# Second cross attention of a four-layer stack: the limits in one VectorE pass, the maximum subtracted on GpSimd, and a new order of the work

## The chip, the cores and the metric

The kernel runs on one core of one Trainium2 chip. The metric is the device time of one execution in microseconds (us). TensorE does the matrix products, VectorE, ScalarE and GpSimd the rest; SyncE issues most transfers. In the rows they are PE (with PEld, its weight loads), DVE, ACT, POOL and SP.

## The reference

A batch of 32 samples with 128 tokens and 256 features goes through four cross attentions (L0 to L3), each followed by a feed-forward part of its own kind. Every attention has 16 heads. The change touches the third of them, which is called L2:

```python
x = x + tanh(g_xattn[2]) * L2_xattn(layernorm(x), ctx_768, ...)

def L2_xattn(query, key_value, ...):          # 16 heads of 16 features, 128 queries, 128 keys
    attn = einsum('bhqd,bhkd->bhqk', q, k) * scale      # scale = 16 ** -0.5
    attn = clip(attn, -10000, 10000)
    attn = softmax(attn, axis=-1)
    attn = where(any(isnan(attn)), 1 / Nkv, attn)
    out  = einsum('bhqk,bhkd->bqhd', attn, v)
    return out @ Wo + bo
```

The L2 feed-forward part is a causal self attention followed by a gated two-matrix part ("self" in the kernel); L3 is another cross attention, with a stack of three residual blocks behind it ("L3f").

## The kernel before

**Lanes and passes.** Four lanes each carry one sample at a time through the stages, in eight passes. The first half of the program runs L0, "bit", L1 and "route" for all passes (FIRST), the second half "mix", L2, "self" and L3 (SECOND). A closing part, L3f, runs eight lanes over four passes. Each lane owns two PSUM pairs of banks and SBUF buffers of its own, so lanes meet only on the engines: each engine takes the steps of all lanes in one fixed sequence, and a step that isn't ready holds up everything behind it on that engine.

**What sets the order.** Each engine's program is a set of generators, one for each lane, that yield after a step. `turns` (a loop over the characters of `ORDER[engine]`) takes the next step of the lane that the next digit names: 0 to 3 are the four lanes, 4 is the set-up work, further characters the eight lanes of L3f. The strings for pe, dve, act, pool and sp have 3,624, 3,963, 3,022, 1,372 and 341 characters. Signals are semaphores that count the steps told, so that the strings may be permuted only between lanes, and every wait holds whatever the order.

**One round of L2.** `dve_heads`, `pool_heads`, `act_heads` and `pe_heads` handle eight heads at a time, two rounds for each sample. In a round TensorE writes the scores of eight heads (line 453 in `pe_heads`, signal s). VectorE takes the maximum of each query and head over the keys (line 796, one instruction over 128x1024 numbers, signal top) and, in L2 alone, clamps these 8 maxima in the small tile `top` (line 800, signal clip). Then for each half c of the round, four heads or 128x512 numbers, three engines follow each other on the tile `t.e[c]` ("big" in the rows):

```python
# VectorE, line 812: max(scores, -limit) - clamped maximum
dve.scalar_tensor_tensor(t.e[half], s8[:, mine, :], -CLAMP / DH ** -0.5, shift, ALU.max, ALU.subtract)
# GpSimd, line 1496: min(that, 0), in place
pool.tensor_scalar(e, e, 0.0, None, ALU.min)
# ScalarE, line 1310: exp(scale * that), in place
act.activation(flat, flat, ACT.Exp, scale=DH ** -0.5)
```

With the minimum against 0 the upper limit is kept: a score above the limit has a clamped maximum equal to the limit. TensorE then transposes the half (line 424), for which it waits for ScalarE's signal p and, at c = 0, for VectorE's second half too. ScalarE copies the transposed halves out of PSUM (line 1269), and after the second round TensorE multiplies by the values (line 469). In "self" and L3 GpSimd has no part in this: VectorE subtracts (line 815) and ScalarE goes on at once. L1's softmax has a GpSimd step of another kind: line 1519 multiplies a 128x512 half by a broadcast reciprocal, tensor by tensor. In all cross attentions and in "self" GpSimd also builds the masked keys (line 1488, 128x512, two instructions for a sample, tensor by tensor), adds a bias to x (line 1506), and computes the norms' reciprocal roots (lines 1471 and 1473; 1527 and 1529 in "self"). On VectorE, line 786 applies a norm, lines 1045, 1052 and 1053 are steps of "self" on 128x256 numbers that lie in SBUF.

Of the kernel before, what the change touches and what calls it, by code (L numbers as in the profile page):

```python
# [10 lines left out]
ALU = mybir.AluOpType  # L11
# [4 lines left out]
P = 128  # L16
# [139 lines left out]
def sequence_a(n):  # L156

    for half in (FIRST, SECOND):
# [8 lines left out]
        "3221131321321342331112232111133212122343200213111300000333021321221011011101033010313313113213200103"  # L167
        "2112123312022323333312132312311222022021233101213001310310032201132331232310132102122331010200031121"
        "1233000302232330220201201332321011301022112102000011100121121102132200130123022033211303302321211002"
        "0022233121213123302031310103011331220321122101201230312323320021031132133000223002303022023321120030"  # L170
        "1002133012202020313113010301101201233033211121100120123022032031131311323300231201021222231322132313"
        "3130333101223102003311221310233210201203232332113131300220200000003320231203301230310302321100322122"
        "1100103303110121112110021012201202303202030331103223312300211002222331212131233133103303122302110220"
        "1303200211031331220102120230003110122100023303223322032031213010013312322023013101301000211333310021"
        "1110211210021023023202030321123123113322312212221213300003122333121232303310123120220331012313321023"
        "0310101221332101311302232020023203202310003123220313211030131030021321010200133020320321120021011212"
        "1200111303201203030310132100300113233223122122101231301301310013033033011223100202231122121201032121"
        "0321200211311332200230030330223320320321012002123011330221212310011303130333120312031203322003301112"
        "1121001201302203020303311020320032122211222213012033113102101023312312320333112032103232113200212012"
        "1332313322002110113000000303302232302320120133001311220202330103113013030012012333130011110211010220"  # L180
        "1230220320311332100200123122322323120120120100131232103200221013313332330101231012021001020203320301"
        "3322123113001102233202032323010101130232311221221033101022322310103102213112001120313323210133120102"
        "1330222213312221332231232313211212313311333121330321200302030112312002300131210012013301301201233023"
        "0031030311122031213030030221130210212020233211301012033123132300132131302201113220303022011130131322"
        "1010213212203103232220112233130032211323010210230132012031123313102000302013313310322032301013212300"
        "2021120133012021320102012003320212300302230021030111301312230201132113232300211201331310012020233020"
        "3102201310310322311322011101013221312001201312320033120120213302022330220231312231230231021030100211"
        "2310013002213120013022330201120123332302021130130312023102132002310111001130230230211003311223200320"
        "1312320033013013210322120223300312011011233103223011102231123120012023332321330022201313021330220203"
        "1312231031021030312003133210031331002233320013322002110321232301122133120301012000323000322130120311"  # L190
        "0311203201132110302301213200101013301032022121112023301303202313221001102212312002323030233021201001"
        "3322213312221330231213013012310100321321003333200232133131002230201132012032321120133010031202103230"
        "0032210320311103112203211032113232311001033123001202010330323103103122011130302231223113300221013231"
        "2330021020331032023222201132223102003031020123323300210013330221302303131022310202133210201300002321"
        "1300213230231310122012103310322023213002120113311320022202233101301122302211301312201213203232310133"
        "0211211220010331121010320302202101231320321132132030110022312313300221331200120012323300330121302103"
        "2032120330031000212330002113001301322130123230321323100103312302221102332031103112320322110101021231"
        "3321032133201111203311120013103212212201330220311023130202113210132313132030322002333220083237287200"
        "328003783789a700a78330a90378a09807a89339873930703a38007098ac97ba908ba98ac0070b7800cab8ca89bc78bc0980"
        "7807acb89ab8c7ba908ba8c07acab7097ba97a890a8ca90bc7070b08a90ab9cb8956bc6b9875c7a6c8c6ab5c965b95ba65cb"  # L200
        "a6c57656ca9565bc9b68756a5c897cb7869685ba95c69c6a6b5a6c5bcabc5976c5b9a6576956597578a68cb659b57c976ca6"
        "5c5bb6ac68c598659b56a5b7a87ca685c6569a565b98b78697c657bc5abc9b6786abca75867568a768b695b7bc5895acb958"
        "6c97c65a6b956575c9b6c565"
    ),
    "dve": (
        "1132322030141341331242424111323324121444144121244111311132202113232313132130230031311212310110111301"
        "3121331233233113032313033100302323230202022020202123322202331112120320200003030311200101030011010011"
        "1220112123331311033303333331011222203323222221122211111110113331212121030131202230131313331313123121"
        "1322121002021222201330303020010100310222221020022322232122320300223323331130303311220022000030030003"
        "1110310200011101100111000010002003201112201113322221331222200211122201110211331331333333332221301111"  # L210
        "2122313300102110121113133000222012222221000120002020233022112331031002233323232322203230130332323323"
        "1103330313312032303200031200000011133111131001112300100202003210010120003301301310022221123222223322"
        "3112100333331333111113202101233311210122111001310313101132321100103332223032323223232010000020020221"
        "1221213322020202321223323002023323131333300323123012302300000000033101303211001111011010121203020020"
        "0001113000333222021112222220022012031331113112111213320331333131312220011013133202111112113312321002"
        "2022212102230030020200203201313221213333330200232232233132000332233213133030313202133000200000002003"
        "0000000031112013101330110110220300012001021000000301022120100020033212230122301222020333113223332331"
        "1310033111011113202211333121211120212122321232132121121001130232012222321210202023230220303030303000"
        "3230111132200022333003103332232333233003131003101000030003300110100120330011101133010100100112202003"
        "2111001110022223320220321122223121211111111022211331313222333131313030133030122111111220200112023332"  # L220
        "2222010000200112032332221210332121032222332233333323000232303013303223331303031333010203230100200032"
        "0030002001311001000011121200101211332011331222112003022022112122233223311002202111033111131132112201"
        "1331313333300130110223131312212112200122013320213200001020202202332101032313213323323230003223213300"
        "0323323232110033313331202300020323000030000101012001030101031101003201321110120201111020223010112122"
        "2313221223220321111222120033303202232331333333132200010222333032002110100300303301122210000123312210"
        "1003033113321211120203330121000021020000000020002000030303022121012333222110311313311330220213111333"
        "0200211121020202331130201131303101221303023230300322321210100033332211212020202333321100013313331133"
        "2223100010122000112133311000220221112232330002021311332302011020012013312100313132020303321111332220"
        "0011113223300121003221323100202001222123130001223202031313103320211012233233020210133213300010213310"
# [1249 lines left out]
def pool_heads(pool, m, t, p, l):  # L1479
# [666 lines left out]
```

## Time and profile before

| | us |
|---|---|
| median of 3 runs | 2675.64 |
| lowest and highest of them | 2671.07 and 2676.82 |
| the profiled execution: its own time | 2694.11 |
| the profiled execution: its span, first to last instruction | 2692.9 |

The profiled execution is 18.5 us longer than the median, and its own time is 1.2 us more than its span. In it TensorE was busy for 2484.1 us, VectorE for 1967.9, ScalarE for 1667.6 and GpSimd for 1327.8. A busy TensorE is not TensorE at its peak, since the ends of matrix products are modelled in the profile. A group of rows gives, for a line, an engine and an operation, the number of instructions, their busy time, the mean of one, and the time that the engine sat idle just before them with what ended it. The chain of waits is followed back from the last instruction, at each step to what released it.

### The profile page before, as it was taken

How to read it: one execution, taken by the hardware profiler on the slowest of the kernel's cores; microseconds unless marked ns; L12 is line 12 of the kernel's file. 1: busy time of each engine (PE TensorE's matmuls, PEld its weight loads, DVE VectorE, ACT ScalarE, POOL GpSimd, SP SyncE). 2: the span in 40 equal slices, each digit the busy share in tenths (PEclk: the TensorE clock that was granted, in tenths of full speed). 3: DMA queues.
4: the chain of work that ended last, by engine and by line, in shares of the span. 5: the costliest groups of instructions: out<-in, count | busy, mean ns of one | idle time of the engine just before them, and what ended most of it. 6: DMA issues, size and time to landing. Idle time of an engine off the chain costs nothing.

```text
span 2692.9 us, 66669 instructions
## 1 busy us (share of the span) xinstructions
PE 2484.1 (92%) x26500; PEld 2026.9 (75%) x26500; DVE 1967.9 (73%) x4666; ACT 1667.6 (62%) x4537; POOL 1327.8 (49%) x2117
## 2 busy tenths in 40 slices
PE   6899989898899999998899989999999989999999
PEld 4777767786677777777677777787777868788887
DVE  7778787869687786966565656667766676668998
ACT  4676767676567667765465555656566565666644
POOL 3232334242544434355664664545545464645777
PEclk9899999999899999999999999999999999999999
DMA  6000000000012221000111221100000000000010
GB/s 197 5 26 8 23 9 21 17 18 15 23 54 60 71 58 41 23 25 17 27 50 50 75 78 31 38 28 19 20 17 20 18 21 18 25 6 25 30 38 28
DMA packets 84191, 92.51 MB, mean 34 GB/s; under 512 B 15333, under 2 KB 77289, under 8 KB 83881
## 3 DMA queue, kind: packets, MB, share of 16 engines
q1 hardware_dynamic: 75432, 59.91, 7.2%
q0 software_dynamic: 8448, 28.34, 3.7%
q8 instruction: 210, 3.44, 0.5%
q14 instruction: 101, 0.82, 0.1%
HBM read 65.36 MB, written 22.85 MB: 33 GB/s over the span
## 4 chain that ended last, share of the span: by engine, by line
PE 48%; DVE 24%; POOL 13%; ACT 9%; issue 4%; DMA 2%; another core or an unknown queue 1%; SPq 0%; DVEq 0%; POOLq 0%; ACTq 0%
PE psum L376 12%; PE psum L369 8%; POOL big L1496 6%; PE psum L404 5%; PE psum L453 5%; DVE tiny L796 4%; PE psum L424 3%; PE psum L597 2%; PE psum L469 2%; ACT big L1310 2%; PE psum L383 2%; PE psum L397 2%; DVE big L815 2%; ACT big L1353 2%; PE psum L591 2%
## 5 line engine op out<-in xcount | busy, mean ns | idle before, releaser
L1310 ACT ACTIVATE big<-big 128x512 f32<-128x512 f32 x512 | 313.1, 630 | 211.3 <-DVE big L815 118.5
L796 DVE TENSOR_REDUCE tiny<-psum 128x8 f32<-128x1024 f32 x256 | 311.7, 1219 | 118.3 <-PE psum L453 112.1
L1471 POOL TENSOR_SCALAR tiny<-mv 128x1 f32<-128x1 f32 x224 | 56.9, 254 | 559.1 <-DVE mv L776 556.8
L424 PEld LDWEIGHTS psum<-ident,big 64*128 64x128 f32 x5120 | 208.6, 141 | 137.7 <-ACT big L1310 72.6
L424 PE MATMUL psum<-ident,big 64*128 64x64 f32 x5120 | 254.4, 232 | 62.2 <-ACT big L1310 41.5
L453 PE MATMUL psum<-head_keys,small 64*128 64x256 f32 x2048 | 286.0, 400 | 21.6 <-POOL head_keys L1488 8.0
L1488 POOL TENSOR_TENSOR head_keys<-big,head_rows 128x512 f32<-128x512 f32 x256 | 267.0, 1052 | 0.2
L815 DVE TENSOR_TENSOR big<-psum,tiny 128x512 f32<-128x512 f32 x384 | 251.3, 682 | 3.4
L1519 POOL TENSOR_TENSOR big<-big,tiny 128x512 f32<-128x512 f32 x128 | 135.1, 1061 | 233.6 <-DVE tiny L851 233.1
L1269 ACT ACTIVATE big<-psum 128x512 f32<-128x512 f32 x384 | 213.1, 600 | 59.7 <-PE psum L424 57.5
L1496 POOL TENSOR_SCALAR big<-big 128x512 f32<-128x512 f32 x128 | 190.8, 1503 | 115.2 <-DVE big L812 115.0
L453 PEld LDWEIGHTS psum<-head_keys,small 64*128 64x128 f32 x2048 | 180.7, 190 | 69.2 <-issue 17.7
L1353 ACT ACTIVATE big<-psum,tiny 128x128 f32<-128x128 f32 x512 | 181.2, 381 | 31.1 <-DVE tiny L846 28.5
L404 PE MATMUL psum<-ident,small 128*128 128x128 f32 x896 | 158.5, 286 | 28.0 <-ACT small L1320 7.7
L1269 ACT ACTIVATE head_keys<-psum 128x512 f32<-128x512 f32 x256 | 141.6, 597 | 47.5 <-PE psum L424 46.6
L786 DVE TENSOR_SCALAR xn<-x,mv,tiny 128x256 f32<-128x256 f32 x192 | 101.1, 528 | 76.1 <-POOL tiny L1473 75.2
L404 PEld LDWEIGHTS psum<-ident,small 128*128 128x128 f32 x896 | 99.6, 142 | 69.2 <-ACT small L1320 15.4
L1473 POOL TENSOR_TENSOR tiny<-tiny,minus_half 128x1 f32<-128x1 f32 x224 | 130.3, 582 | 18.7
L369 PE MATMUL psum<-xnT,w_L 128*128 128x128 f32 x1024 | 132.1, 280 | 1.1 <-ACT xnT L1340 0.5
L369 PEld LDWEIGHTS psum<-xnT,w_L 128*128 128x128 f32 x1024 | 126.3, 195 | 6.6 <-issue 2.8
L369 PE MATMUL psum<-xnT,w_up 128*128 128x128 f32 x1024 | 129.8, 278 | 0.0
L597 PE MATMUL psum<-w_L,head_keys 128*128 128x256 f32 x512 | 128.3, 389 | 0.8 <-ACT head_keys L1362 0.5
(340 smaller groups left out, 6638.1 us busy)
## 6 DMA issues: line engine op xcount, KB each, us to landing
ctxT<-in_ctxT SPq DMA_DIRECT2D x64, 128.0 KB, 2.2
after_L_xattn<-x SPq DMA_DIRECT2D x64, 128.0 KB, 1.7
mixture_out<-spare SPq DMA_DIRECT2D x46, 128.0 KB
x_in<-in_x SPq DMA_DIRECT2D x32, 128.0 KB
mixture_in<-xn SPq DMA_DIRECT2D x32, 128.0 KB, 1.7
x_in<-after_L_xattn SPq DMA_DIRECT2D x32, 128.0 KB
w_bits<-after_L_xattn SPq DMA_DIRECT2D x32, 128.0 KB, 2.2
spare<-in_L_w SPq DMA_DIRECT2D x2, 1024.0 KB, 6.4
```

What stands on the lines that cost most here:

```text
L369: last = pe.matmul(bank[:, j * S:(j + 1) * S], wt[:, k, n * P:(n + 1) * P], src[:, k, :], start=k == 0, stop=k == KD - 1)
L376: last = pe.matmul(bank[:, 0:n], srcT[:, k, :], wt[:, k, 0:n], start=k == 0, stop=k == chunks - 1)
L404: last = pe.transpose(bank[:, k * P:(k + 1) * P], src[:, k * P:(k + 1) * P], identity)
L424: last = pe.transpose(t.ab[:, half, at:at + P // 2], t.e[c][rows, j, :], m.ident[rows, rows])
L453: last = pe.matmul(t.ab[:, half, cols], t.qT[rows, r, :], keys[rows, cols], start=l != "self", stop=l != "self" or cols.start > 0)
L796: dve.tensor_reduce(top, s8, AX.X, ALU.max).then_inc(*t.dve.tell(p, f"{l}.top{r}"))
L815: dve.tensor_tensor(t.e[half], s8[:, mine, :], shift, ALU.subtract).then_inc(*t.dve.tell(p, f"{l}.e{2 * r + half}"))
L1269: return act.activation(dst.rearrange("p h (r s) -> p h r s", r=2), src, ACT.Copy)
L1310: last = act.activation(flat, flat, ACT.Exp, scale=DH ** -0.5)
L1353: last = act.activation(t.e[half][:, j, :], t.ab[:, half, j * S:(j + 1) * S], ACT.Exp, scale=WIDE ** -0.5, bias=t.tiny[:, 8 + h:9 + h], ac ...
L1488: pool.tensor_tensor(t.head_keys[r], t.kT[:, r:r + 1, :].to_broadcast([P, CH, S]), m.head_rows[:].rearrange("p (h o) -> p h o", o=1).to_br ...
L1496: pool.tensor_scalar(e, e, 0.0, None, ALU.min).then_inc(*t.pool.tell(p, f"{l}.below{c}"))
```

## The change

In L2 alone VectorE's pass keeps both limits and no longer subtracts: it takes max(score, -limit) and then the minimum of that and the clamped maximum. GpSimd's step takes two tensors instead of a tensor and a constant: it subtracts the clamped maximum, which is read from the small tile and broadcast over the keys. The number of instructions and the signals stay the same. The order strings of all five engines are other ones; every step of every lane is still there.

```diff
 ORDER = {
     "pe": (
-        "3221131321321342331112232111133212122343200213111300000333021321221011011101033010313313113213200103"
...
+        "2311323312131224111332231121313212123243202011311300020030321313201011012111300301313131131233021030"
...
@@ dve_heads
             if l == "L2":
-                dve.scalar_tensor_tensor(t.e[half], s8[:, mine, :], -CLAMP / DH ** -0.5, shift, ALU.max, ALU.subtract
+                dve.scalar_tensor_tensor(t.e[half], s8[:, mine, :], -CLAMP / DH ** -0.5, shift, ALU.max, ALU.min
                                          ).then_inc(*t.dve.tell(p, f"{l}.e{2 * r + half}"))
@@ pool_heads
     if l == "L2":
         for c in range(4):
-            e = t.e[c % 2].rearrange("p h s -> p (h s)")
+            top = t.tiny[:, 8 + CH * (c % 2):8 + CH * (c % 2 + 1)].rearrange("p (h o) -> p h o", o=1)
             pool.wait_ge(*t.dve.at(p, f"{l}.e{c}"))
-            pool.tensor_scalar(e, e, 0.0, None, ALU.min).then_inc(*t.pool.tell(p, f"{l}.below{c}"))
+            pool.tensor_tensor(t.e[c % 2], t.e[c % 2], top.to_broadcast([P, CH, S]), ALU.subtract
+                               ).then_inc(*t.pool.tell(p, f"{l}.below{c}"))
             yield
```

Of the steps, the places in the strings differ like this: on TensorE 1,463 of 3,624 stand elsewhere, mostly by one or two places and by 11 at most; on GpSimd 882 of 1,372, by 15 at most, and on SyncE by up to 18. The changes are spread over the whole program, not over L2 alone. The added line moves the lines behind it by one, so that 1506 is now 1507, 1527 now 1528 and 1609 now 1610, while the changed GpSimd instruction is still at line 1496.

**Place 1: TensorE, second round of L2 of lane 0 in an early pass.** A number behind a name is the lane. Before, from the scores of lane 0 (line 453, head_keys_0) to the transposes of both its halves (line 424, big_0) and on:

```order
L453 MATMUL psum<-head_keys_0,small_0 128x256 x4
L424 MATMUL psum<-ident,big_1 128x64 x16
L369 MATMUL psum<-xnT_2,w_up 128x128 x8
L424 MATMUL psum<-ident,big_3 128x64 x16
L453 MATMUL psum<-head_keys_1,small_1 128x256 x4
L469 MATMUL psum<-big_3,small_3 32x128 x8
L469 MATMUL psum<-head_keys_3,small_3 32x128 x8
L424 MATMUL psum<-ident,big_0 128x64 x16
L404 MATMUL psum<-ident,small_3 128x128 x4
L376 MATMUL psum<-w_down,big_2 128x256 x6
```

Of the change, the same stretch:

```order
L453 MATMUL psum<-head_keys_0,small_0 128x256 x4
L424 MATMUL psum<-ident,big_1 128x64 x8
L369 MATMUL psum<-xnT_2,w_up 128x128 x8
L424 MATMUL psum<-ident,big_3 128x64 x8
L453 MATMUL psum<-head_keys_1,small_1 128x256 x4
L424 MATMUL psum<-ident,big_3 128x64 x8
L376 MATMUL psum<-w_down,big_2 128x256 x3
L469 MATMUL psum<-big_3,small_3 32x128 x8
L469 MATMUL psum<-head_keys_3,small_3 32x128 x8
L376 MATMUL psum<-w_down,big_2 128x256 x3
L404 MATMUL psum<-ident,small_3 128x128 x4
L424 MATMUL psum<-ident,big_1 128x64 x8
```

Behind the last of these rows stand the halves of lane 0, one at a time, with a half of lane 1 between them. The six products with w_down and the four transposes of small_3 now stand between lane 0's scores and its transposes, where they came behind these before.

**Place 2: GpSimd, the same round of lane 0.** Before:

```order
L1554 TENSOR_TENSOR tiny_2<-tiny_2 128x1
L1488 TENSOR_TENSOR head_keys_1<-big_1,head_rows 128x512
L1496 TENSOR_SCALAR big_0<-big_0 128x512 x2
L1506 TENSOR_TENSOR x_1<-x_1,out_bias_L3 128x256
L1506 TENSOR_TENSOR x_0<-x_0,out_bias_L2 128x256
L1609 DMA yg_1<-mixture_out0,token_place0 128x256
```

Of the change:

```order
L1530 TENSOR_TENSOR tiny_2<-tiny_2,minus_half 128x1
L1496 TENSOR_TENSOR big_0<-big_0,tiny_0 128x512
L1507 TENSOR_TENSOR x_1<-x_1,out_bias_L3 128x256
L1610 DMA yg_1<-mixture_out0,token_place0 128x256
L1496 TENSOR_TENSOR big_0<-big_0,tiny_0 128x512
L1507 TENSOR_TENSOR x_0<-x_0,out_bias_L2 128x256
```

The two halves of lane 0 stood back to back; now a bias and the issue of an indirect transfer stand between them. Over the program 7 of the 64 pairs had other work between their halves, and now 6 have.

**Place 3: TensorE at the start of the program, in L0, which the two edits don't touch.** Before:

```order
L404 MATMUL psum<-ident,xn_1 128x128 x2
L404 MATMUL psum<-ident,xn_3 128x128 x2
L404 MATMUL psum<-ident,xn_2 128x128 x2
L369 MATMUL psum<-xnT_1,w_L0q 128x128 x4
L369 MATMUL psum<-xnT_3,w_L0q 128x128 x4
L369 MATMUL psum<-xnT_2,w_L0q 128x128 x4
```

Of the change:

```order
L404 MATMUL psum<-ident,xn_3 128x128 x2
L369 MATMUL psum<-xnT_3,w_L0q 128x128 x4
L404 MATMUL psum<-ident,xn_1 128x128 x2
L404 MATMUL psum<-ident,xn_2 128x128 x2
L369 MATMUL psum<-xnT_1,w_L0q 128x128 x4
L453 MATMUL psum<-head_keys_3,small_3 128x256 x4
```

Lane 3 now goes ahead of lane 1, and the scores of lane 3 come ahead of lane 2's queries.

## Rows read from the trace of the kernel before

**Rows 1.** The page's first part and its row of TensorE's granted clock in 40 slices.

```profile
PE 2484.1 (92%) x26500; PEld 2026.9 (75%) x26500; DVE 1967.9 (73%) x4666; ACT 1667.6 (62%) x4537; POOL 1327.8 (49%) x2117
...
PEclk9899999999899999999999999999999999999999
```

**Rows 2.** Busy time by windows: stretch, its length, PE, PEld, DVE, ACT, POOL, granted clock.

```profile
0.00:1157.00 1157.00, 1047.31 (x11848) 844.53 (x11849) 910.01 (x2379) 774.50 (x2362) 435.31 (x689) 0.96 0.13 39
1157.00:2400.00 1243.00, 1150.30 (x12702) 944.88 (x12702) 804.36 (x1560) 730.98 (x1777) 699.06 (x1032) 0.99 0.11 31
2400.00:2693.00 293.00, 286.51 (x1954) 237.46 (x1952) 253.51 (x728) 162.07 (x399) 193.41 (x398) 1.00 0.09 28
```

**Rows 3.** TensorE's waits, 1157 to 2400: total us, times, longest.

```profile
PE psum L424 <- ACT big L1310: 34.3, 57, 1.0
...
PE psum L404 <- DVE small L1045: 7.1, 8, 2.1
PE psum L404 <- DVE xn L786: 5.7, 7, 1.8
```

**Rows 4.** The chain of waits by line, 1157 to 2400.

```profile
by line: POOL big L1496 12.9%; PE psum L376 10.9%; PE psum L369 8.6%; PE psum L453 7.7%; DVE tiny L796 7.1%; PE psum L404 5.1%; issue 4.3%; PE psum L424 4.0%; ACT big L1310 3.2%; PE psum L469 3.0%; DVE big L812 2.8%; POOL head_keys L1488 2.
```

**Rows 5.** Line 1496's own instructions, and ScalarE's waits for it, 1157 to 2400.

```profile
L1496 POOL TENSOR_SCALAR big<-big x128: 1475/1496/1750, 1167.4 to 2398.8; 128x512 f32<-128x512 f32 x128
...
ACT big L1310 <- POOL big L1496: 90.8, 102, 2.7
```

**Rows 6.** Timeline: start, us, instruction, idle before it; place 1 and 2 before.

```profile
1456.69 0.69 DVE L812 SCALAR_TENSOR_TENSOR big<-psum,tiny 128x512 f32<-128x512 f32 x1
...
1457.47 2.96 POOL L1496 TENSOR_SCALAR big<-big 128x512 f32<-128x512 f32 x2 [0.84 <-DVE big L812]
...
1460.45 0.63 ACT L1310 ACTIVATE big<-big 128x512 f32<-128x512 f32 x1 [0.82 <-POOL big L1496]
...
1461.14 0.46 PE L424 MATMUL psum<-ident,big 64*128 64x64 f32 x8 [0.83 <-ACT big L1310]
```

**Rows 7.** GpSimd's groups: line 1519 from the page, the others 1157 to 2400.

```profile
L1519 POOL TENSOR_TENSOR big<-big,tiny 128x512 f32<-128x512 f32 x128 | 135.1, 1061 | 233.6 <-DVE tiny L851 233.1
...
L1488 POOL TENSOR_TENSOR head_keys<-big,head_rows 128x512 f32<-128x512 f32 x184 | 191.5, 1050 | 0.2
L1496 POOL TENSOR_SCALAR big<-big 128x512 f32<-128x512 f32 x128 | 190.8, 1503 | 115.2 <-DVE big L812 115.0
...
L1506 POOL TENSOR_TENSOR x<-x,out_bias_L 128x256 f32<-128x256 f32 x60 | 44.1, 738 | 0.3
```

**Rows 8.** The longest of line 1519, and VectorE's passes over 128x512 scores.

```profile
L1519 POOL TENSOR_TENSOR big<-big,tiny x128: 1031/1041/1397, 93.9 to 1209.7; 128x512 f32<-128x512 f32 x128
...
L815 DVE TENSOR_TENSOR big<-psum,tiny 128x512 f32<-128x512 f32 x235 | 153.8, 681 | 2.2
L812 DVE SCALAR_TENSOR_TENSOR big<-psum,tiny 128x512 f32<-128x512 f32 x128 | 84.7, 685 | 1.7
```

**Rows 9.** VectorE on SBUF operands: groups of 1157 to 2400, then least, median, most.

```profile
L786 DVE TENSOR_SCALAR xn<-x,mv,tiny 128x256 f32<-128x256 f32 x96 | 53.2, 554 | 47.2 <-POOL tiny L1473 46.8
...
L1053 DVE SCALAR_TENSOR_TENSOR x<-xn,gates,x 128x256 f32<-128x256 f32 x30 | 19.1, 635 | 0.0
L1052 DVE TENSOR_SCALAR small<-xn,tiny 128x256 f32<-128x256 f32 x30 | 17.9, 598 | 19.6 <-POOL tiny L1529 19.5
...
L786 DVE TENSOR_SCALAR xn<-x,mv,tiny x192: 321/412/1240, 53.1 to 2496.8; 128x256 f32<-128x256 f32 x192
...
L1052 DVE TENSOR_SCALAR small<-xn,tiny x32: 325/354/1232, 1249.0 to 2469.6; 128x256 f32<-128x256 f32 x32
...
L1053 DVE SCALAR_TENSOR_TENSOR x<-xn,gates,x x32: 472/480/1257, 1249.2 to 2469.9; 128x256 f32<-128x256 f32 x32
```

**Rows 10.** Timeline of one such pass beside GpSimd's masked keys.

```profile
1408.91 1.05 POOL L1488 TENSOR_TENSOR head_keys<-big,head_rows 128x512 f32<-128x512 f32 x1
...
1408.93 1.17 DVE L1052 TENSOR_SCALAR small<-xn,tiny 128x256 f32<-128x256 f32 x1 [0.78 <-POOL tiny L1529]
```

More of the change, by code:

```diff
@@ L172 @@
[L172 to L181, printed above, removed]
@@ new lines @@
+        "1002103310222210303113010301101201203313321112100120120322032031131313133223012010022221133222132133"
+        "1033303312123102001331221310233210102203232332131131230020200000003230213120330213032030321100221221"
+        "1001303330110121112100112012201202303202030331031223312300101222203312121213233133103303122302112200"
+        "1303200211031231320102120230003110122100023303232320203232101301013312232012301301013001013323310021"
+        "1121021110021032023202030311223121123223321232121231300020312313212233303310123120220331103123321023"
@@ new lines @@
+        "0310101221332101311302232020020233023201003122320313211030310130032112010020133020320121320012021121"
+        "1200111303201203030310132100300123123323121222101231031301310013030330311322100202213122121201302121"
+        "3021200231101122330203030330223323020312012002123011332021221301011331330303120312031203322003301121"
+        "2111001201302302020303321012030032132112222221301230113101012230312312233330112303213022311200212012"
+        "1332313322002110113030000003302232301232012033001312102202331010313013030001123333100211102112100120"
@@ new lines @@
+        "1230223020311332100203102122322321312020120100131321203200230112313332330112031012210010020203320301"
+        "3322123131300211230202032323110010013232311221221033101022322310101302231112001120231023331133120102"
+        "3130222233112221332232323113211212313311333121332120300030032112310023200311210021013301031202133203"
+        "0030030131221131321300030220311201212020233211310010323123132230131031302201113220303022011130131322"
+        "1010213212323310202221012231323231010323010210230123010231123313010200300213313312032032300113212300"
@@ new lines @@
+        "2021102313021021230102020023312032310002230201310101302321130201132113232301201201331301021020233020"
+        "3103122031130122301322011101013221312001230321210303021120231302220331020223312231023120301230100211"
+        "2010313002213121003302230201120123303232032110312312003120123230010111010130230230121003311223200320"
+        "3123210033013013021321220322310301101013232013223011102231123210012023332321330022201313021330202201"
+        "3312312013001303210032331021033300221313320013232032112012032301121332013201002100233000322101320311"
@@ new lines @@
+        "0311203201132110302301213200101301301032022121113202301303202312231001102231232100232013023302201003"
+        "1322233112221330231213013013201210023133300332201021331312002330201123012302321120133010031202012330"
+        "0032210203113131122030211032113232310101033123001202010330321301303220101131320233123230011022112332"
+        "1330021020331032023222201132223102003031002133232300210013332201303203131022310202133210201300002121"
+        "3302132032113031022012031310322023213002121103311320022202233110301122302211301312201213203323120133"
@@ new lines @@
+        "0211112200213031122100331020120201213320321132132030110032210021333322131200120012323320201330123010"
+        "3032120330003100122000123310031301322131230230323231001013312302221102332031103112320322110101021231"
+        "3321321330121101203311123001203122121233010220311023103202113210132313132030030223020332238237287200"
+        "32800378387a007a873390a90837a9078098337a983903703a83008790a7c0a9b8c89aba0009800bac78b78cac8bc9b70987"
+        "087a0bc8a8b9c7ab9b80ca8ac7a09b7078a9ba7a009c8a9c70b70b80a90acb98b596c6b85897bc6a7c65cab69cb5956ba5cb"
@@ new lines @@
+        "2102111323312311333033033303111222203322321212222121111011113331122211031301202230131313333131213211"
+        "1322121010202222102330030302001100310222221020022232123222320200333223331131330103220022000300000031"
+        "1130013201101010101101010000002320001021121113322223113222202011122021101211313331133333333222301111"
+        "2221333100102101211113311130002220222222010020002020233022112321013030233223233232203021330332323323"
+        "1310033133312302330320001020101000133110311211310100010020203020102110003300131310022221132323222221"
@@ new lines @@
+        "2113210033131133333011322102131312120231111001131033011121213310030332220332322222310000322000302021"
+        "1221213322022002312232332020023323131333300321323103023200000000033113013120011011111010021023020000"
+        "2001110300323223021112222022220201031331113111121120233331313331123220011011303322112112111231233021"
+        "2212020012230030200200202313103221213333330002223232231233030032323213130330133220133000200000300200"
+        "0000000000132111030310111112320130200100021000030010202121000200032312031223210222002333113223333323"
@@ new lines @@
+        "1313100111013111202211333121210112121232212321232121121001310232012223221201002322320323020030030030"
+        "3230113122100032233030103332232333233003131001303100000003300010112010313010103001013010110112020120"
+        "3120101110022223032220321212322111221111111222110133313222333313103031313030122111111222000120232332"
+        "2221010002020110323322211223031201032232322233333323000223303013303223333303013130301203201000200203"
+        "0333000011120100010111002211001021330211331012221023022202121133222232311002220111301111313132112333"
@@ new lines @@
+        "1033133312131001010112123332122112200212202330113200100020022202332101032313213333330002223322213320"
+        "0203323323110333031331220300232300000030001001210100031100101103001320132101120201111022203101120122"
+        "2223123123221021311222120033330202233233313133313220000222333030202101100303003301122210000132322101"
+        "0031031313322210101123330212002001000010000202000000033322021120100333222113103111313303222011313310"
+        "0302211112000322331120012113303102122002331303033032221210010033332211212020220333312100013313313133"
@@ new lines @@
+        "2022310010100202211133311022000221121233302202011013323020311021002330213001131310203230321111332220"
+        "0011113332200211022030013123122000223221130102032220303111303023211102233323200201123333100103301210"
+        "2023133100312321113200001122000021112333202011212200303302202033112213003011122233113000221121100232"
+        "3011101332202302323112011010121232302300111003322232001011233200032223332320101333130122230313031000"
+        "1113223211100010323323320020021321133220021131303020000022133213130001331132122330003332221113120021"
@@ new lines @@
+        "1112303223201213003031011022221001330220223111333030011221000333322110202021313330100110222313000012"
+        "3332321130100022212003233200200010112023030322121132311313000113322321313200202331311130022111012330"
+        "3220101220330310121222101002322320313113330202101122233332020101333300101330001303321321321100002232"
+        "3113101000223332002120121320232000023022113123330003230021210333322120101131330220200112112323030021"
+        "1113322220030301313222231111001022333322220002333131122002111303222000333113301221221001001132321230"
```

180 lines of the change are left out of this document (65 added, 115 removed).

## The prediction

> **What bounds the kernel now.** I read the page's busy shares first. TensorE is busy for 2484.1 us, VectorE for 1967.9, GpSimd for 1327.8 [rows 1]. TensorE is the fullest engine, but no engine is full, so the question is where TensorE stands still. Its granted clock reads nine tenths in 38 slices of 40 and eight in two, that is, the 2.4 GHz level nearly throughout, and I expect nothing from it [rows 1].
>
> The windows split the program where L2 begins and ends. From 1157 to 2400 us TensorE is busy for 1150.3 of 1243 us: it idles 92.7 us there. It idles 109.7 us before that and 6.5 us after [rows 2]. GpSimd has 699 us of work in the stretch, far from full.
>
> The list of waits says what ends those 92.7 us. The greatest item is the transposes waiting for ScalarE's exponentials: 34.3 us in 57 waits, the longest 1.0 us; the next are 7.1 and 5.7 us, for VectorE passes [rows 3]. Behind ScalarE stands GpSimd: ScalarE waited 90.8 us for line 1496, in 102 cases [rows 5]. The chain of waits agrees: line 1496 is its largest item in this stretch, 12.9%, or 160 us. At 1.503 us each that is 107 of the 128 halves [rows 4, 7].
>
> One place shows the mechanism. VectorE ends the first half at 1457.38, GpSimd takes 2.96 us for the two halves back to back, ScalarE gets the second at 1460.45 and TensorE its transposes at 1461.14 after 0.83 us idle [rows 6]. So the GpSimd step is latency on the softmax loop of L2, not load.
>
> **The change part by part.** *The GpSimd step.* Removed: 128 instructions of tensor and constant at 1503 ns. Added: 128 of tensor and tensor, the second broadcast from the small tile. The nearest row is line 1519, the same shape with the same kind of broadcast, a multiplication: 1061 ns; line 1488, another broadcast pair, takes 1050 [rows 7]. The longest of line 1519 took 1397 ns, against 1475 for the shortest of line 1496 [rows 5, 8], so even the dear end is a small saving. I take 1061: 0.442 us less for a half, 56.6 us of GpSimd time in all. What counts is when the halves are ready: the first 0.44 us sooner, the second, queued behind it, 0.88.
>
> The Trainium skill speaks against this edit (GPSIMD Engine Reference, Engine selection, and Performance versus the Vector engine): it calls one-input work on GpSimd roughly line-rate and two-input work slow, at some 2.6 cycles an element for a pair and 1.8 for a tight loop; as an estimate from that page a half would rise from 768 ns to 1109, and 128 halves would cost 44 us more GpSimd time. The trace bears out the pair (1061) and not the one-input form (1503), and the measurement decides.
>
> *What TensorE gets of it.* If each of the 57 waits lost 0.44 us, that is 25 us; if all vanished, 34.3. Some belong to "self" and L3, where GpSimd has no part, and the row doesn't part them. Since TensorE waits for both halves and the second gains 0.88 us, more than the mean wait of 0.60, I take **28 us** of idle time removed. Not all is kept: TensorE arrives earlier at its next steps, and some aren't ready yet (the VectorE passes of rows 3 are the next late). I count three quarters: **-21 us**. The ends are nothing kept, and a chain that shortens at every one of its 107 halves: 107 x 0.442 = 47 us.
>
> *The VectorE pass.* The same instruction with a minimum for a subtraction. Line 812 takes 685 ns, line 815 681 for a subtraction alone [rows 8]; 128 times their difference is 0.5 us. I cost it at nothing.
>
> *The shared port.* A VectorE pass whose operands lie in SBUF stands still beside a GpSimd pair: line 1052 took 1.17 us beside line 1488 instead of its median 0.354 [rows 9, 10]. In this stretch line 786 averages 554 against a median of 412 ns (96 times, 13.6 us), line 1052 598 against 354 (30 times, 7.3 us), line 1053 635 against 480 (30 times, 4.7 us): 25.6 us in all, beside 235.6 us of large GpSimd pairs (191.5 + 44.1) [rows 7, 9]. The change adds 128 x 1.061 = 135.8 us of pairs, in proportion 14.8 us of VectorE stalls. VectorE has 439 us idle there [rows 2], and of TensorE's waits few are for these lines. I take **+2 us** on the path, between 0 and 14.8. The Trainium skill (GPSIMD Engine Reference, Key points) says the same of the interfaces that GpSimd shares with VectorE instructions of two SBUF inputs or a 2-port mode; by that rule the trace agrees.
>
> *The order.* In place 1 six products and four transposes now fill TensorE between lane 0's scores and its transposes, where it stood idle for 0.83 us; but in place 2 a bias (0.738 us, rows 7) and a transfer's issue now part the two halves on GpSimd, so that the second half isn't sooner there at all. The same steps are permuted, by one or two places as a rule; a step put behind another lane's delays every step behind it, DMA issues on GpSimd and SyncE too. No row prices this. I take **-2 us**; the bounds are a third of TensorE's idle time outside the stretch, 116.2 / 3 = 39 us, either way.
>
> *Sum.* -21 + 2 - 2 = -21 us. The profiled execution took 2694.1 us, so 2673.1 in its like. The median of the runs is 18.5 us lower, 2675.64; there the sum gives **2655 us**, 0.8% less. Some 0.2% (5.4 us) is what a measurement of this kernel can tell from no change.
>
> **The rivals.**
>
> *More is kept.* The chain runs through 107 of 128 halves, and an order laid for the shorter step could keep each 0.44 us: 2675.6 - 47 = 2629, or some 2636 with the port's share and a few losses. Against it: TensorE has only 92.7 us of idle time there, in small waits of many kinds.
>
> *Absorbed.* Either the pair with a subtraction is dearer than the one with a multiplication, near the 1397 ns end (then 0.106 us is saved for a half, a quarter of the sum: the change doesn't do what it says), or the next late step (VectorE's passes of rows 3) takes the place of the exponentials. A quarter of 28 us less the port's 2 us leaves 5: 2671. For it: TensorE's order is fixed, and the waits are short. Against it: no other item of rows 3 is near 34.3.
>
> *The port.* All 14.8 us fall on the path, because line 786 stands ahead of TensorE's transposes of xn: -21 + 14.8 - 2 = -8, 2667. For it: TensorE already waits for line 786 and line 1045, 12.8 us together [rows 3].
>
> *The order loses: slower.* One mechanism: in stages that the two edits don't touch, as in place 3, steps of two lanes have changed places on engines that run in order, and a step late on the chip now stands ahead of one that is ready. TensorE idles 116.2 us outside the stretch [rows 2]. The gain is gone when that grows by 18% (21 us), and it is slower by more than 0.2% from 23% on (27 us). A third more gives -21 + 2 + 39 = +20, 2696. For it: 1,463 steps of TensorE's moved all over the program. Against it: moves of one or two places among steps mostly ready, and a TensorE busy for 91% of the first part.
>
> **How the numbers follow.** The forecast (10 to 35 us gained) has 0.55; more than that 0.10; absorbed 0.12; the port 0.10; the order loses 0.13. The predicted time is that of the forecast. The range runs from 2633, most of the first rival, to 2681, where "slower" begins: it leaves out the far part of the first rival, some 0.05, and nearly all of the last, 0.12. Faster by over 0.2%: 0.55 + 0.10 and of absorbed and port some 0.10 together, 0.75. Within 0.2%: the rest of those two and a little of the last, 0.13. Slower: 0.12.
>
> **What the profile after should show.** Line 1496 as a tensor pair at about 1061 ns, 128 times; line 812 still near 685 ns. ScalarE's waits for line 1496 well under 90.8 us, TensorE's for line 1310 between L2's start and end down from 34.3 us to some 10, and its idle time there from 92.7 to about 70. Line 1496's share of the chain falls by more than its duration. Line 786's mean in the L2 part rises above 554 ns. Outside that part TensorE's idle time stays within a few us of 116. The prediction is wrong if the pair takes over 1.3 us, if TensorE's other waits grow by as much as those for ScalarE fall, or if the untouched first part gets longer or shorter by over 15 us.

## The result, and the profile after

| | us |
|---|---|
| the change, median of 3 runs | 2615.70 (2609.94 to 2615.98) |
| before, median of 3 runs | 2675.64 |
| ratio, 95% interval | 0.9772 (0.9756 to 0.9788) |
| predicted | 2655, range 2633 to 2681 |

The change is 59.9 us faster, 2.3%. The direction was right; the forecast of 21 us was about a third of it, and the time lies below the range. The profiled execution of the change took 2615.7 us, its median, while that of before was 18.5 us over its own. The profiles alone would give 78 us, so differences between these two profiles are too large; verdicts below rest on ratios of runs on the same chip.

The first part of the page, the windows of the three parts of the program (their bounds are L2's first and last GpSimd step), and TensorE's and ScalarE's waits in the middle one:

```profile
PE 2461.5 (94%) x26500; PEld 2020.3 (77%) x26500; DVE 1966.0 (75%) x4666; ACT 1667.1 (64%) x4539; POOL 1269.9 (49%) x2117
```

```profile
0.00:1152.00 1152.00, 1050.28 (x11987) 849.00 (x11987) 916.47 (x2392) 780.90 (x2388) 443.24 (x699) 0.96 0.13 40
1152.00:2321.00 1169.00, 1123.08 (x12555) 933.19 (x12552) 793.91 (x1548) 722.18 (x1750) 630.80 (x1020) 1.00 0.11 33
2321.00:2614.00 293.00, 288.11 (x1964) 238.14 (x1963) 255.64 (x728) 164.05 (x402) 195.81 (x400) 1.00 0.09 28
```

```profile
PE psum L404 <- DVE xn L786: 7.8, 7, 1.9
PE psum L424 <- ACT big L1310: 6.8, 17, 2.1
PE psum L404 <- DVE small L1052: 5.6, 7, 2.4
...
ACT big L1310 <- POOL big L1496: 49.4, 65, 4.2
```

Beside [rows 2], TensorE's idle time in the middle part is 45.9 us instead of 92.7. The greatest wait of [rows 3], 34.3 us in 57 cases, is 6.8 us in 17, and ScalarE's waits for line 1496 fell from 90.8 us [rows 5] to 49.4. In the chain of waits of that part line 1496 has 3.9% instead of 12.9% [rows 4]:

```profile
by line: PE psum L376 14.3%; PE psum L369 14.1%; PE psum L453 9.7%; PE psum L404 6.9%; PE psum L424 5.7%; PE psum L469 4.9%; DVE tiny L796 4.9%; POOL big L1496 3.9%; issue 3.4%; DVE big L815 2.4%; DMA mixture_out<-spare 1.7%; ACT big L1310 
```

The groups of the two edited lines (the same part) answer to [rows 7, 8]: the pair takes 1047 ns, VectorE's pass 684.

```profile
L1496 POOL TENSOR_TENSOR big<-big,tiny 128x512 f32<-128x512 f32 x128 | 131.8, 1047 | 123.3 <-DVE big L812 123.2
...
L812 DVE SCALAR_TENSOR_TENSOR big<-psum,tiny 128x512 f32<-128x512 f32 x127 | 83.5, 684 | 1.7
```

Places 1 and 2 in the timeline after the change, to be held against [rows 6]:

```profile
1427.10 0.68 DVE L812 SCALAR_TENSOR_TENSOR big<-psum,tiny 128x512 f32<-128x512 f32 x1
...
1427.86 1.04 POOL L1496 TENSOR_TENSOR big<-big,tiny 128x512 f32<-128x512 f32 x1 [9.42 <-DVE big L812]
1428.86 0.74 POOL L1507 TENSOR_TENSOR x<-x,out_bias_L 128x256 f32<-128x256 f32 x1
...
1429.55 0.68 DVE L812 SCALAR_TENSOR_TENSOR big<-psum,tiny 128x512 f32<-128x512 f32 x1
1429.75 1.02 POOL L1610 DMA_INDIRECT yg<-mixture_out,token_place  x1 [0.16 <-DVE big L815]
...
1430.80 1.05 POOL L1496 TENSOR_TENSOR big<-big,tiny 128x512 f32<-128x512 f32 x1
```

The same stretch of TensorE:

```profile
1429.81 1.56 PE L376 MATMUL psum<-w_down,big 128*128 128x256 f32 x6
1431.21 0.60 PE L404 MATMUL psum<-ident,small 128*128 128x128 f32 x4
1431.74 1.30 PE L424 MATMUL psum<-ident,big 64*128 64x64 f32 x32
```

The second half is ready 4.1 us after VectorE's first half (1431.85 less 1427.78), later than the 3.05 us of before. The greater part of that is VectorE's: its own second half ends only at 1430.23, 2.45 us after the first, because the new order puts other passes between the two. The transfer's issue holds GpSimd for another 0.57 us. Even so TensorE shows no idle time before the transposes: the products with w_down stand where it had waited for 0.83 us.

### The profile page after: what moved, and what is told of

The parts are those of the page before. It is cut to its first block, busy times and chain, and to the rows that moved or that the text cites. A ratio compares the mean times of both kernels' runs of the same rounds, so it can differ in the third digit from the quotient of the medians.

```text
span 2614.5 us, 66673 instructions
## 1 busy us (share of the span) xinstructions
PE 2461.5 (94%) x26500; PEld 2020.3 (77%) x26500; DVE 1966.0 (75%) x4666; ACT 1667.1 (64%) x4539; POOL 1269.9 (49%) x2117
## 4 chain that ended last, share of the span: by engine, by line
PE 57%; DVE 22%; POOL 8%; ACT 7%; issue 4%; DMA 2%; SPq 0%; DVEq 0%; POOLq 0%; ACTq 0%
PE psum L376 12%; PE psum L369 11%; PE psum L453 6%; PE psum L404 6%; PE psum L424 5%; DVE tiny L796 3%; PE psum L469 3%; PE psum L597 3%; PE psum L383 2%; PE psum L397 2%; DVE big L815 2%; PE psum L390 2%; ACT big L1353 2%; POOL big L1496 2%; PE psum L591 2%
## 5 line engine op out<-in xcount | busy, mean ns | idle before, releaser
L1520 POOL TENSOR_TENSOR big<-big,tiny 128x512 f32<-128x512 f32 x128 | 134.8, 1058 | 218.8 <-DVE tiny L851 218.6
L1496 POOL TENSOR_TENSOR big<-big,tiny 128x512 f32<-128x512 f32 x128 | 131.8, 1047 | 123.3 <-DVE big L812 123.2
```

## The experiments

The runs came in three groups, each on one chip beside runs of before: 1 to 4 (before: 2673.2 us), 5 to 8 (2697.9 us) and 9 to 12 (2695.3 us). A ratio is against before in the same group. The numbers are those of the headings below. Theories A and B of runs 1 to 4 ask whether the edit or the order gives most; those of runs 7 and 8 ask how far the step's length is felt, and are theories of their own.

**1. The edit alone.** The lines of the change, the strings of before.

```diff
-ORDER = { ...the change's strings }
+ORDER = { ...the strings of before }
```

> Both edited lines, with the order strings of before. Theory A (the softmax loop of L2 ran at the pace of the GpSimd step, the edit itself gives most): 2635 us or less, at least 40 us under before. Theory B (the new order gives most): the recorded sum for the edit alone, some 19 us under before, 2657 us. Theory C (the edit is worth its full bound, 107 halves by 0.442 us, the order nothing): 2628 us.

Measured: 2633.82 us against 2673.16, ratio 0.9848 (0.9831 to 0.9864), 39.3 us faster. Theory A holds: it is under its 2635 us, if 0.7 us short of its "at least 40". Theory B's 2657 falls, theory C's 2628 is missed by 6 us, and my sum for the edit, 19 us, is half of what was measured. The windows and waits of its middle part:

```profile
1160.00:2338.00 1178.00, 1127.49 (x12556) 932.80 (x12549) 800.25 (x1548) 721.74 (x1749) 632.12 (x1021) 1.00 0.11 33
```

```profile
PE psum L453 <- POOL head_keys L1488: 9.2, 8, 2.2
PE psum L404 <- DVE small L1045: 8.4, 11, 2.0
PE psum L404 <- DVE xn L786: 6.3, 8, 1.4
PE psum L424 <- ACT big L1310: 5.4, 15, 0.6
```

TensorE's waits for the exponentials fell from 34.3 us to 5.4, 28.9 us, the 28 us of my sum to within one. But the whole idle time fell by more, from 91.1 us (1232 less the 1140.92 of the row below, before over the same part) to 50.5 us, and the waits that I expected to grow in their place grew little: line 1045's is 8.4 against 7.1, line 786's 6.3 against 5.7 [rows 3], line 1488's 9.2 against 7.3.

```profile
1167.00:2399.00 1232.00, 1140.92 (x12568) 937.39 (x12559) 797.80 (x1548) 722.66 (x1749) 690.80 (x1021) 0.99 0.11 31
```

By these two rows the middle part alone is 54 us shorter, while the kernel gained 39.3: the profiled execution of before was a slow one, and the difference in idle time is too large for it. Runs 5 and 6, on one chip, are the fairer pair.

**2. The order alone.** The lines of before, the strings of the change.

```diff
-ORDER = { ...the strings of before }
+ORDER = { ...the change's strings }
```

> The two lines of before, with the order strings of the change. Theory A: not far from before, 2660 to 2680 us, since the GpSimd step still takes 1.50 us. Theory B: most of the 60 us, 2640 us or less. If the order was laid for the short step and loses with the long one, over 2680 us.

Measured: 2657.72 us, ratio 0.9945 (0.9929 to 0.9962), 15.4 us faster. It is 2 us under the range that theory A gave, and 18 us above theory B's bound. The two parts are nearly independent: 39.3 + 15.4 = 54.7 of the 59.9 us, and the product of the ratios, 0.9794, lies 0.0022 above 0.9772, which intervals of 0.0016 either way for each ratio can't tell from nothing.

**3 and 4. The new order in one half of the program.** The edit, with the new strings up to the end of the first half and the old ones behind (3), and the reverse (4). Both orders have given every lane the same number of steps at the five places of the cut.

```diff
-    "pe": new
+    "pe": new[:1532] + old[1532:]      # 3; old[:1532] + new[1532:] in 4
```

> Both edited lines; the new order up to the end of the first half (pe 1532 characters, dve 1973, act 1315, pool 509, sp 152), the old order behind it. In the profiles L2's first GpSimd step starts 15.5 us sooner after the change (1151.9 against 1167.4). If that comes of the order, this is 10 to 16 us faster than the edit with the old order throughout; if it was a slower profiled execution, within 5 us of it.

> Both edited lines; the old order up to the end of the first half, the new order behind it. If the first half's gain is of the order, this is 10 to 16 us slower than the change, 2626 to 2632 us; if not, within 5 us of 2615.7. Theory B wants this at least 25 us faster than the edit with the old order; theory A within 15 us of it.

Measured: 2622.37 us, ratio 0.9816 (0.9798 to 0.9833), and 2623.37 us, 0.9815 (0.9798 to 0.9831). Against the edit alone the first half's order gives 11.4 us and the second half's 10.5; both are in the change, whose ratio is lower still. Run 3 meets its expectation of 10 to 16 us. Run 4 is 7.7 us slower than the 2615.7 us of the change, between the two cases that I had named, but 0.0043 by ratios, 11.5 us, which is the first of them. The new order's gain is spread over the program, also over stages without any edit. So the fourth rival named the right place with the wrong sign. In the first part of the program, the windows of run 1 and of run 3:

```profile
0.00:1160.00 1160.00, 1052.70 (x11987) 850.11 (x11987) 916.33 (x2391) 781.57 (x2388) 441.91 (x699) 0.97 0.13 39
```

```profile
0.00:1146.00 1146.00, 1042.19 (x11971) 843.66 (x11975) 915.30 (x2391) 780.75 (x2388) 443.54 (x698) 0.97 0.13 40
```

The part is 14 us shorter, but TensorE's idle time only 3.5 us (107.3 to 103.8); the rest is busy time. The profiled execution of run 1 was the slowest of its four (2634.5 us) and that of run 3 the fastest (2620.2), so about 3 of the 14 us are no gain of the order. How much of the busy time is the clock and which exchanges of steps do the rest stays open. The order of a single engine wasn't tried.

**5. Before once more**, unchanged, for a second profile.

> The kernel before, unchanged, for a second profile of it: the first was 18.5 us over its median. Expected: a span near 2675 us, L2's first GpSimd step at 1160 us rather than 1167.4 (where the edit with the old order has it, over identical work), and its last about 1222 us later rather than 1231.

Measured: 2699.78 us, with before's other runs on that chip at 2697.87. The expectation failed: this chip is slower throughout, and the execution looks like the first profiled one of before, with L2's first step at 1172.6 us and its last 1232.2 us later (1231.4 there). So there is no profile of before at its 2673 us. Its middle part is the base for runs 6 to 8:

```profile
1173.00:2405.00 1232.00, 1143.58 (x12550) 939.47 (x12549) 798.75 (x1547) 722.76 (x1749) 690.49 (x1021) 0.99 0.11 31
```

**6 and 10. A short step with one input.**

```diff
-            pool.tensor_scalar(e, e, 0.0, None, ALU.min).then_inc(...)
+            pool.tensor_scalar(e[:, 0:325], e[:, 0:325], 0.0, None, ALU.min).then_inc(...)
```

> The kernel and order of before, with GpSimd's minimum over the first 325 of 512 columns only (the upper limit isn't applied to the rest), so that a half takes about 1.05 us as the new pair does, but with one tensor input. If the pair's second input costs VectorE nothing that counts: as the edit with the old order, 2634 us within 5. If the pairs stall VectorE on the path by the 14.8 us of the recorded bound: 2619 us.

> The one-input step of about 1.04 us with the old order once more, on the same chip as the tensor pair of about 1.05 us. If the pair's second input costs nothing on the path: within 0.001 of edit_old_order_2. If the ratios of the two earlier jobs (0.9825 and 0.9848) told a cost of the pair: 0.002 below it, some 6 us.

The step took a median of 1.036 us:

```profile
L1496 POOL TENSOR_SCALAR big<-big x128: 1013/1036/1211, 1174.4 to 2357.4; 128x325 f32<-128x325 f32 x128
```

Measured first: 2651.97 us, ratio 0.9825 (0.9812 to 0.9838), 0.0023 below run 1, which was on another chip. So both went on one chip.

**9. The edit alone, again.** The kernel of run 1.

> Both edited lines with the old order once more, to stand on one chip beside the next run. 0.9848 of before again, within 0.0015.

Measured: run 9 2654.59 us, ratio 0.9841 (0.9822 to 0.9861); run 10 2653.08 us, 0.9836 (0.9818 to 0.9854). They differ by 1.5 us, or 0.0005, inside both intervals; taken together these leave room for some 7 us either way. Run 9 repeats run 1's 0.9848 within the 0.0015 expected, and the 0.0023 between runs 6 and 1 doesn't come back on one chip. What the edit brings is the duration of the step; that it now reads two tensors costs the kernel nothing that these runs can tell.

**7. No step on GpSimd.** ScalarE waits for VectorE's pass.

```diff
-                if l == "L2":
-                    act.wait_ge(*t.pool.at(p, f"{l}.below{c}"))
-                else:
-                    act.wait_ge(*t.dve.at(p, f"{l}.e{c}"))
+                act.wait_ge(*t.dve.at(p, f"{l}.e{c}"))
@@ pool_heads: the instruction and its signals are gone
```

> The kernel and order of before, without GpSimd's step in L2 (the upper limit isn't applied; ScalarE waits for VectorE's pass). Theory A (the step is serial on a loop that sets the pace, at the 0.67 us a us that the edit with the old order showed): 2675 less 0.67 x 192 = 129 us, 2546 us. Theory B (the time lay in TensorE's waits for these exponentials, 32.5 us in the stage before and 5.3 with the edit in the old order): no more than 10 us under the edit, 2624 us or more.

Measured: 2645.25 us, ratio 0.9805 (0.979 to 0.982), 52.6 us under before. Theory A predicted 129 and falls here. Theory B allowed 10 us more than the edit: it is 9.7 us by the ratios against run 9, 11.5 against run 1 and 5.4 against run 6, so it holds about at its limit. Taking the last 1.04 us away gives only 6.7 us more than run 6 on the same chip.

**8. The step twice.**

```diff
+            pool.tensor_scalar(e, e, 0.0, None, ALU.min).then_inc(*t.pool.tell(p, f"{l}.half{c}"))
+            pool.wait_ge(*t.pool.at(p, f"{l}.half{c}"))
             pool.tensor_scalar(e, e, 0.0, None, ALU.min).then_inc(*t.pool.tell(p, f"{l}.below{c}"))
```

> The kernel and order of before, with the minimum taken twice for each half: the GpSimd step takes 3.0 us instead of 1.5. Theory A: 0.67 to 1 of 128 x 1.5 = 192 us, so 2804 to 2868 us. If slack in the order takes some of it: less than 100 us over before.

Measured: 2980.41 us, ratio 1.1045 (1.1029 to 1.1062): 282.5 us slower, more than the 192 us that the added instructions last, and beyond both expectations (129 to 192 us, or under 100).

```profile
1170.00:2688.00 1518.00, 1267.80 (x12565) 1032.01 (x12563) 796.68 (x1548) 724.67 (x1748) 877.03 (x1148) 0.89 0.09 25
```

```profile
PE psum L424 <- ACT big L1310: 179.6, 102, 3.2
```

```profile
PEclk8999999998999999889898899898989989989999
```

Against run 5 the middle part is 286 us longer. TensorE's idle time rose from 88.4 to 250.2 us, by 162; its busy time rose by 124 us for the same products. In the windows the granted clock fell from 0.99 to 0.89. Equal work at that ratio would be 1143.6 x 0.99 / 0.89 = 1272 us, and 1267.8 was measured. That takes the mean of the window for the clock of the busy time. The clock's records in the two traces allow the count itself: of TensorE's busy time 289 us lie in stretches granted 1.2 GHz, the lower of its two levels, against 23 us in run 5, and half of the 266 us more is 133 us. So the clock accounts for all of the 124 us, as an estimate: TensorE stood still more often, and worked more of the time at the lower level.

**11. The change, again,** beside runs 9, 10 and 12.

> The change itself on the same chip: 0.9772 of before, within 0.0015, so 0.007 to 0.008 below the edit with the old order.

Measured: 2631.97 us, ratio 0.9756 (0.9736 to 0.9777), 22.6 us under the edit with the old order (run 9), or 0.0085; a little more than the 0.007 to 0.008 expected.

**12. No step, with the new order.**

> The GpSimd step left out (the upper limit isn't applied) with the new order. If the step's latency has stopped setting the pace, as in the old order, where leaving it out gave only 0.2% more than a step of 1.04 us: no more than 8 us under the change. If the new order runs tight on it: 20 us or more under the change.

Measured: 2623.61 us, ratio 0.9739 (0.9713 to 0.9765), 8.4 us under the change, about the 8 us allowed if the step no longer sets the pace. The intervals overlap and its five runs spread over 15 us, so that this isn't told from no gain. It leaves out the upper limit, so it isn't a version to use. None of the runs that keep the computation beat the change.

Put in a row, for the old order and in us on the chip of runs 5 to 8, the length of the step and the time are as follows (run 10 has -42.2 for 1.04 us on another chip):

```
GpSimd step of a half    us to before (2698 us chip)
none                     -52.6
1.04 us                  -45.9
1.50 us (before)            0
3.00 us                 +282.5
```

## Why the prediction was wrong

**What bounds the kernel: right, for a part of the step.** The step was latency on L2's softmax loop. Runs 6, 9 and 10 show that its duration alone does it; run 7 shows that of 1.50 us hardly more than the last 0.46 counted.

**"I take 1061": right.** 1047 ns, and VectorE's pass unchanged at 684 to 685.

**"28 us of idle time removed": right as a count of that wait.** It fell from 34.3 to 5.4 us in run 1.

**"Not all is kept ... I count three quarters": this step failed.** All of it was kept, and 11 us on top: 39.3 us against 28. Three things are seen in its place. First, TensorE's idle time fell by more than its waits for the exponentials: by 34.0 us between runs 5 and 6 on one chip (1232 - 1143.6 and 1183 - 1128.6, rows of run 5 and below), where those waits fell by 28.7. So the other waits didn't take the place of these, they fell too, by 5 us in sum. I read it so: a wait at the end of a lane's loop delays the other lanes' steps on every engine that works in order, so its price isn't in its own row alone. That is argued; no run parts it. (Between before and run 1 the idle time fell by 40.6 us, with the slow profile of before in it.) Second, TensorE's busy time in the middle part fell by 15.0 us between runs 5 and 6 (1143.6 to 1128.6), with the same products. By the traces 23 us of it lay at 1.2 GHz in run 5 and 8 in run 6, which makes some 8 of the 15 us the clock, as an estimate; the prediction had put the clock at nothing. The remainder isn't settled. The profile models the ends of products, so a burst before a wait may be shown longer than it works, and there are fewer waits; this is an argument, not shown. Third, the bound of 47 us from the chain of waits held: 107 halves by 0.442. It was nearer than my sum, and I had it only as an end.

```profile
1174.00:2357.00 1183.00, 1128.55 (x12556) 932.88 (x12548) 792.67 (x1546) 721.04 (x1746) 633.29 (x1020) 1.00 0.11 33
```

The waits of these two windows, run 5 and then run 6:

```profile
PE psum L424 <- ACT big L1310: 34.1, 58, 1.0
```

```profile
PE psum L424 <- ACT big L1310: 5.4, 16, 0.5
```

**The shared port, "+2 us": not contradicted, and too small to be seen.** Run 1's groups in the middle part, against [rows 9]:

```profile
L786 DVE TENSOR_SCALAR xn<-x,mv,tiny 128x256 f32<-128x256 f32 x94 | 54.4, 578 | 39.1 <-POOL tiny L1473 38.7
L1053 DVE SCALAR_TENSOR_TENSOR x<-xn,gates,x 128x256 f32<-128x256 f32 x30 | 20.5, 685 | 0.0
L1052 DVE TENSOR_SCALAR small<-xn,tiny 128x256 f32<-128x256 f32 x30 | 17.7, 591 | 16.7 <-POOL tiny L1530 16.4
```

The means moved from 554 to 578, 635 to 685 and 598 to 591 ns. The sum is 54.4 + 20.5 + 17.7 = 92.6 us. [Rows 9] give 90.2, with two passes of line 786 more in their window; over 1167 to 2399, with the same 94, it is 88.6. So 4.0 us more of VectorE time rather than 14.8. The fairest pair is runs 9 and 10, where steps of one length differ in their second tensor (and line 812, at 0.684 us in both, in its operation):

```profile
1172.00:2360.00 1188.00, 1133.74 (x12568) 936.58 (x12561) 801.14 (x1548) 721.70 (x1751) 633.14 (x1022) 0.99 0.11 33
```

```profile
1171.00:2357.00 1186.00, 1133.19 (x12579) 937.65 (x12568) 793.97 (x1549) 722.70 (x1751) 634.77 (x1023) 0.99 0.11 33
```

The pairs cost VectorE 7.2 us there (801.14 less 793.97), half of the 14.8, and the kernel 1.5 us, which is within noise. The third rival, all 14.8 us on the path, falls, since the two runs leave room for 9 us at most. The stall itself is real [rows 10]; but its growth in proportion to the time of GpSimd pairs wasn't: what counts is which pass meets a pair, and few met the halves of L2. Of line 786's passes only 12 began under line 1496 in run 9, at a mean of 0.698 us; before, 13 began under it as a one-input step, at 0.446, where 0.407 is the mean of those with nothing on GpSimd beside them.

**The order, "-2 us": failed.** With the old lines it gave 15.4 us (run 2), with the new ones 18.1 (2633.8 to 2615.7, or 20.3 by the ratios) and 22.6 on the other chip. It lay inside the bound of 39 us either way. But I carried that bound only to the side of a loss, as a rival; on the side of a gain it would have taken the range down to 2618 us (2655 + 2 - 39), and with the chain's 47 us further. Of the 2.3% some two thirds are the edit and a third the order. Why the new order gains is not shown; the runs show only that it does so in both halves, and as a whole with the old lines too.

**The rivals.** "More is kept" was the right one, with 0.10. Its 2636 us is what the edit alone gives (0.9848 of 2675.6 is 2635), and it stopped there, since the order's gain wasn't in it. "Absorbed" and "the port" fall with runs 1, 9 and 10. That the first part would stay as it was is wrong: run 3 is 11.4 us faster than run 1.

**The signs.** The pair's 1047 ns, ScalarE's 49.4 us and the 6.8 us of TensorE's waits for line 1310 came as expected. TensorE's idle time in the middle part fell to 45.9 us, not 70, and outside it to 106.6 (101.7 and 4.9) from 116. Line 786's mean didn't rise above 554 ns in the change: it is 520. L2's first step came 15.5 us sooner (1151.9 against 1167.4), just over the 15 us that I had named as a sign of being wrong, though in part because the profile of before was slow.

## What to carry to other kernels

A wait of the fullest engine that the chain of waits shows again and again can be worth more than the sum of that engine's waits for it: here the waits were 34.3 us and the gain 39 to 46. For a small cut, work out the chain's count of links too (47 us here), and count down only for what is seen to be late next. For a large cut that count is far too high: 107 halves by the whole 1.503 us are 161 us, and leaving the step out gave 52.6. Ask how long the latency can be before it is hidden: here there was next to nothing to gain below 1.04 us, 46 us between 1.04 and 1.50, and more than one for one above. An order laid anew for a shorter step is an edit of its own; price it by the idle time in all of the program, and give the range both ends. And look whether the profiled execution is like the median before comparing two profiles.

## What the runs showed of the hardware

- GpSimd took 1.50 us for the minimum of 128x512 numbers and a constant, and 1.05 us for the difference of 128x512 numbers and a broadcast operand. The one-input form over 325 columns took 1.04 us, 3.2 ns a column against the pair's 2.0.
- The one-input form and the pair, at equal duration, gave the same time of the kernel within noise: 2653.1 and 2654.6 us (runs 10 and 9). VectorE was busy for 7.2 us less in the middle part beside the one-input form.
- Passes of line 786 that began under line 1496 took 0.446 us on average while it was a one-input step (13 of them) and 0.698 while it was a pair (12), against 0.407 with nothing on GpSimd beside them.
- A TensorE that waited for 250 us in a part of 1518 us was granted 0.89 of its clock there, against 0.99 with 88 us in 1232 us. Its busy time was 124 us longer for the same products, beside 162 us more of waits.
- The same kernel took 2673 us on one chip, 2695 on a second and 2698 on a third.
